# Two graph attention layers in one kernel: h1 stored by columns, deeper h and output buffers, an earlier start of the sparse rows

## The reference

```
h  = relu(layernorm(x))                       # layer 0
Wh = h @ W
e  = (Wh @ a[:256])[:, None] + (Wh @ a[256:])[None, :]
x  = x + leaky_relu(softmax(where(adj == 0, -1e9, e), axis=1) @ Wh, 0.2)
h  = relu(layernorm(x))                       # layer 1
h1, h2 = h @ a1[:256], h @ a1[256:]
e  = leaky_relu(h1 + h2.T, 0.01)
x  = x + softmax(where(adj > 0, e, -9e15), axis=1) @ h
```

## Time and profile before

| | |
|---|---|
| median of three runs | 1716.38 us |
| profiled execution | 1716.22 us |
| its span | 1714.0 us |
| end of layer 0, start of layer 1 | 1068.7 us |
| busy over the span | PE 91%, DVE 73%, ACT 58%, POOL 33% |
| mean granted TensorE clock | 0.966 of full speed |

### The profile page before, as it was taken

One profiled execution on the slowest core, in us unless ns is written; L12 is line 12 of the kernel. 1 busy time (PEld: TensorE's weight loads), 2 busy tenths in 40 slices (PEclk: granted clock), 3 DMA queues, 4 the chain that ended last, 5 costly groups with the idle time before them and its releaser, 6 DMA issues. The chain is left out here.

```text
span 1714.0 us, 37172 instructions
## 1 busy us (share of the span) xinstructions
PE 1559.3 (91%) x13443; PEld 1327.4 (77%) x13443; DVE 1258.1 (73%) x4759; ACT 992.5 (58%) x1514; POOL 557.3 (33%) x588
## 2 busy tenths in 40 slices
PE   6877999999999999999999997585599999899877
PEld 5646888888888888888888886464488888787666
DVE  7577998998899889987864443596676766666556
ACT  5878656665666566657666641675454444444342
POOL 0000000000000000000035561576677777777774
PEclk9998999999999999999999999897799999999989
DMA  9418989988988898889899973745444444444433
GB/s 315 165 44 346 352 299 340 345 309 306 363 329 298 311 367 318 299 316 377 325 343 398 388 277 79 165 133 143 111 133 123 129 117 133 116 139 117 127 110 91
DMA packets 141698, 406.89 MB, mean 237 GB/s; under 512 B 25857, under 2 KB 91586, under 8 KB 108834
## 3 DMA queue, kind: packets, MB, share of 16 engines
q1 hardware_dynamic: 116114, 335.11, 53.5%
q0 software_dynamic: 25488, 70.77, 14.8%
HBM read 365.39 MB, written 40.41 MB: 237 GB/s over the span
## 5 line engine op out<-in xcount | busy, mean ns | idle before, releaser
L1006 PE MATMUL banks<-HV,adjT 128*128 128x257 f16 x8192 | 940.0, 274 | 16.6 <-DVE adjT L665 9.1
L1006 PEld LDWEIGHTS banks<-HV,adjT 128*128 128x128 fp8e4 x8192 | 793.3, 98 | 148.5 <-DVE HV L695 22.9
L1746 PE MATMUL banks<-Vp,adjp 128*128 128x257 f16 x2304 | 454.2, 279 | 97.2 <-DVE adjp L1560 79.8
L450 ACT ACTIVATE adj_f<-adj_i 128x2048 fp8e4<-128x2048 int32 x256 | 480.2, 1897 | 5.4 <-DMA adj_i<-in_adj 5.1
L1331 POOL DMA_INDIRECT gat<-h_of_layer,rec x393 | 415.0, 1056 | 149.3 <-issue 111.4
L1746 PE MATMUL banks<-Vn,adjn 128*128 128x257 f16 x2304 | 453.6, 279 | 0.0
L1746 PEld LDWEIGHTS banks<-Vp,adjp 128*128 128x128 fp8e4 x2304 | 226.0, 99 | 142.7 <-DVE Vn L1520 64.9
L432 POOL DMA_DIRECT2D xr<-x_after_layer x46 | 26.3, 572 | 832.4 <-DVE rank L933 772.3
L1746 PEld LDWEIGHTS banks<-Vn,adjn 128*128 128x128 fp8e4 x2304 | 228.8, 99 | 37.9
L1367 ACT ACTIVATE adjn<-h1bc,nh 128x384 fp8e5<-128x384 f32 x384 | 205.0, 605 | 35.5 <-PE banks L1746 31.1
L1619 DVE SCALAR_TENSOR_TENSOR sacc<-gat,w,sacc 128x257 f32<-128x257 f32 x347 | 156.7, 478 | 0.0
(11 more groups left out here) (172 smaller groups left out, 1484.3 us busy)
## 6 DMA issues: line engine op xcount, KB each, us to landing
adj_i<-in_adj SPq DMA_DIRECT2D x256, 1024.0 KB, 7.0
h_of_layer<-hh SPq DMA_DIRECT2D x64, 129.0 KB, 6.3
hs<-h_of_layer SPq DMA_DIRECT2D x64, 129.0 KB, 2.7
xt<-in_x SPq DMA_DIRECT2D x64, 128.0 KB, 6.7
packed_adj<-pk SPq DMA_DIRECT2D x64, 128.0 KB, 6.1
x_after_layer<-x SPq DMA_DIRECT2D x64, 128.0 KB, 6.6
HV<-in_x SPq DMA_DIRECT2D x14, 512.0 KB, 8.8
gat<-h_of_layer,rec POOLq DMA_INDIRECT x393, 2.8
```

What stands on the lines that cost most here:

```text
L450: nc.scalar.activation(adj_f[:, b, q * QC:(q + 1) * QC], adj_i[:, q, :], ACT.Copy, scale=2.0, saturate=False).then_inc(conv_done, 1)
L1006: last = nc.tensor.matmul(acc[b][:, 0:DV], adjT_h[:, b, i, q, :, h], V0[:, jb, s, 0:DV], start=(jb == 0 and s == 0), stop=(jb == T - 1 and ...
L1746: mm = nc.tensor.matmul(bank[2 * i + part][:, 0:DV], m[:, i * P:(i + 1) * P], V[:, j, s, 0:DV], start=(j == 0 and s == 0), stop=(j == T - ...
```

## The change

In layer 0 `store_h` also stores the tile's column of `h1all`, 128 numbers from 128 partitions, to its row of `h1_d`; layer 0 ends only when all 64 have landed. Layer 1 has no transpose, copy and store of h1 any more; its first transfer is the broadcast of h1 for group 0. `HS` goes from 4 to 8: eight tiles of h are loaded at the start (two share a semaphore), and later ones two chunks ahead instead of one. `NOUT` goes from 4 to 6. `HEAD` goes from 1.0 to 0.25, so three rows stand in the loop of chunk 1 and five in those that follow. For chunk 0 the low halves and the weights of the own rows come before the first masks, and ACT's Exp for those weights before the first signs; for later chunks the order stays.

```diff
                 def store_h(t, off, b):
                     sp.wait_ge(h12_kept, 3 * t + 3)
                     sp.dma_start(h_rows(t + off), hh[:, b, :]).then_inc(hh_out[b], 16)
+                    sp.dma_start(h1_d[t + off, :].rearrange("(p o) -> p o", o=1), h1all[:, t + off:t + off + 1])\
+                        .then_inc(h1_out, 16)
...
                 sp.wait_ge(rec_in, 16)
+                sp.wait_ge(h1_out, 16 * T)
...
-        HS = 4
+        HS = 8
...
-        HEAD = 1.0
+        HEAD = 0.25
         OUT_LAG = 5
-        NOUT = 4
+        NOUT = 6
...
-                for b in range(HS):
-                    sp.dma_start(hs[:, b, :], h_rows(tiles[b])).then_inc(h_in[b], 16)
+                load_h1(0, 0)
+                for b in range(CB):
+                    sp.dma_start(hs[:, b, :], h_rows(tiles[b])).then_inc(h_in[b // 2], 16)
                 load_words(0, 0)
+                for b in range(CB, HS):
+                    sp.dma_start(hs[:, b, :], h_rows(tiles[b])).then_inc(h_in[b // 2], 16)
                 load_words(0, 1)
-                sp.wait_ge(h1T_sb, 1)
-                sp.dma_start(h1_d, h1T[:, :]).then_inc(h1_out, 16)
-                sp.wait_ge(h1_out, 16)
-                load_h1(0, 0)
                 load_h1(1, 1)
...
-                    if g == 0 and c < NC - 1:
-                        for t in range((c + 1) * CB, (c + 2) * CB):
+                    if g == 0:
+                        for t in range(c * CB + HS, min(T, (c + 1) * CB + HS)):
                             sp.wait_ge(v_ready, 2 * (t - HS) + 2)
-                            sp.dma_start(hs[:, t % HS, :], h_rows(tiles[t])).then_inc(h_in[t % HS], 16)
+                            sp.dma_start(hs[:, t % HS, :], h_rows(tiles[t])).then_inc(h_in[t % HS // 2], 16)
...
                 halves(0)
+                act.wait_ge(wself_ready, 2)
+                nc.scalar.activation(zself[:, :, :], zself[:, :, :], ACT.Exp).then_inc(wself_ready, 1)
                 signs_of(0)
                 signs_of(1)
                 halves(1)
                 act.wait_ge(hb_ready, 2)
-                act.wait_ge(wself_ready, 2)
-                nc.scalar.activation(zself[:, :, :], zself[:, :, :], ACT.Exp).then_inc(wself_ready, 1)
...
-                nc.vector.tensor_copy(h1T[:, :], bank[7][0:T, 0:P]).then_inc(h1T_sb, 1)
...
+                    if n == 0:
+                        for t in range(CB):
+                            low_halves(t, t % HS)
+                        self_weights()
                     negatives(n, g, c)
-                    if g == 0:
-                        low_halves(c * CB, 0)
+                    if g == 0 and n > 0:
+                        low_halves(c * CB, c * CB % HS)
                     positives(n, c)
-                    if g == 0:
+                    if g == 0 and n > 0:
...
                 prepare(0)
-                self_weights()
...
-                nc.tensor.transpose(bank[7][0:T, 0:P], h1all[:, :], idf[:, :]).then_inc(h1T_ps, 1)
```

More of the change, by code:

```diff
@@ L302, in two_layer_graph_attention @@
             rec_in = sem("rec_in")
+            h1_out = sem("h1_out")
             x1_out = [sem(f"x1_out{i}") for i in range(NX)]
@@ L1118, in two_layer_graph_attention @@
             tM = early[:, 6 * T:7 * T]
-            h1T = early[0:T, 7 * T:7 * T + P]
             sS = early[:, 9 * T:9 * T + 2 * NS].rearrange("p (s t) -> p s t", s=2)
@@ L1143, in two_layer_graph_attention @@
             fac = cnt[:, 4 * G:6 * G].rearrange("p (s g) -> p s g", s=2)
-            h_in = [sem(f"h_in{i}") for i in range(HS)]
+            h_in = [sem(f"h_in{i}") for i in range(HS // 2)]
             pkg_in = [sem(f"pkg_in{i}") for i in range(2)]
@@ L1148, in two_layer_graph_attention @@
             x1g_in = sem("x1g_in")
-            h1T_ps = sem("h1T_ps")
-            h1T_sb = sem("h1T_sb")
-            h1_out = sem("h1_out")
             exc_ready = sem("exc_ready")
@@ L1348, in _ @@
                 act.wait_ge(dM_ready, 2)
-                act.wait_ge(h1T_ps, 1)
                 nc.scalar.activation(ab[:, :, :], dM[:, :, :], ACT.Exp).then_inc(ab_ready, 1)
@@ L1353, in high_halves @@
                 def high_halves(t, j, n_in):
-                    act.wait_ge(h_in[j], n_in)
+                    act.wait_ge(h_in[j // 2], n_in)
                     for s, V in ((0, Vp), (1, Vn)):
@@ L1409, in halves @@
                     for j in range(CB):
-                        high_halves(c * CB + j, j % HS, (c * CB + j) // HS * 16 + 16)
+                        t = c * CB + j
+                        high_halves(t, t % HS, t // HS * 32 + 32)
                 def signs_of(n):
@@ L1462, in _ @@
             def _(dve):
+                nc.vector.tensor_scalar(nh2[:, :], h2all[:, :], -BIG, None, ALU.mult)\
+                    .then_inc(nh2_ready, 1)
                 nc.vector.tensor_tensor(exc[:, :], rec_f[:, :, DEG], capv[:, :], ALU.subtract).then_inc(exc_ready, 1)
@@ L1467, in _ @@
                 nc.vector.reduce_max(red_in[:, 2:3], exc[:, :], AX.X).then_inc(mx_ready, 1)
-                dve.wait_ge(h1T_ps, 1)
-                nc.vector.tensor_copy(h1T[:, :], bank[7][0:T, 0:P]).then_inc(h1T_sb, 1)
-                nc.vector.tensor_scalar(nh2[:, :], h2all[:, :], -BIG, None, ALU.mult)\
-                    .then_inc(nh2_ready, 1)
                 dve.wait_ge(M_all, 1)
@@ L1661, in prepare @@
                         unpack(n, g, c, n >= 2 * UB)
+                    if n == 0:
+                        for t in range(CB):
+                            low_halves(t, t % HS)
+                        self_weights()
                     negatives(n, g, c)
-                    if g == 0:
-                        low_halves(c * CB, 0)
+                    if g == 0 and n > 0:
+                        low_halves(c * CB, c * CB % HS)
                     positives(n, c)
-                    if g == 0:
-                        for j in range(1, CB):
-                            low_halves(c * CB + j, j % HS)
+                    if g == 0 and n > 0:
+                        for t in range(c * CB + 1, c * CB + CB):
+                            low_halves(t, t % HS)
                 def self_weights():
@@ L1737, in group @@
                                     if j == 0:
-                                        if first and i == 0 and part == 0:
-                                            pe.wait_ge(h1T_sb, 1)
                                         if not first:
```

## The result

The changed kernel takes **1805.0 us** (median of four runs, 1794.97 to 1810.58), 1.0508 times the kernel before on the same chip [1.046, 1.0555]. Forecast were 1687.3 us. The change is slower by 5%, and the prediction is wrong.

What follows compares the result with a forecast made beforehand. The prediction took POOL to bound layer 1 from 1232 to about 1690 us, with PE full in layer 0's fullest stretch. From 1716.22 us, -27.2 + 8.2 + 0.7 - 2.6 - 8 = -28.9 gave 1687.3 us, range 1672 to 1704.

Steps and rivals of the forecast that it cites:

- The cost in layer 0: Layer 0's 64 added column stores: taken as 0 because PE never waits, upper bound 7 us.
- The end of layer 0: Last column store is one issue and one landing later than the last h: +0.7 us (0.4 to 1.5).
- if layer 0 ends more than 2 us later: Sign at the end of layer 0 that would show the forecast wrong.
- POOL's stops: Layer 1's first group: POOL's seven stops for DVE to free a gather buffer go away, -27.2 us.
- Rows from chunk 0: Layer 1's first group: earlier rows and eight h buffers remove POOL's 10.98 us stop.
- SyncE's blocks: Layer 1's first group: output buffer waits at L1226 stay, but the third holds nothing up; DVE loses some 10 and 4 us.
- The others under 8: Sign in layer 1's first group: ACT's 16.5 us wait for h gone, its other waits under 8 us.
- The price of the fuller DVE: Layer 1's first group: gathers take longer beside a denser DVE, +8.2 us.
- The rival with 2.5 us for a gather and its gap: Layer 1's first group: DVE's unbroken runs block POOL throughout, ending at 1728.9 us; chance 5%.
- The start and the change of group: Layer 1: PE starts some 1.5 us earlier, and its group 1 at 1200 to 1208 us instead of 1232.
- The tail: End of layer 1: six output buffers remove two late POOL stops, -2.6 us, and bring the last sums earlier, -8 us.
- the likeliest case: Whole kernel: the forecast itself, 1687.3 us with its own range 1678 to 1698; chance 65%.

Runs made afterwards that it cites:

- e6: Kernel before plus one extra store per layer 0 tile, 128 pieces of 32 bytes without gaps; 1714.37 us, ratio 0.9992.
- e4: Kernel before plus one extra store per layer 0 tile, 128 pieces of 512 bytes without gaps; 1712.65 us, ratio 0.9996.
- e10: Kernel before plus one extra store per layer 0 tile, 128 pieces of 4 bytes, 32 bytes apart; 1712.68 us, ratio 0.9998.
- e2: Changed kernel without the column stores; h1 goes to DRAM through the transpose on PE, as before; 1685.86 us, ratio 0.9843.
- e9: As e2, but with four h buffers (HS 4) as before; 1699.07 us, ratio 0.9896.
- e8: As e2, but with HEAD 1.0 as before; 1686.72 us, ratio 0.984.
- e7: As e2, but with four output buffers (NOUT 4) as before; 1695.24 us, ratio 0.989.
- e15: Kernel before plus a store per layer 0 tile: 128 4-byte pieces filling one 512-byte row, neighbours written 16 pieces apart; 1766.34 us, ratio 1.0309.
- e1: Kernel before plus the column store of h1 in layer 0, 128 pieces of 4 bytes without gaps per tile; 1809.14 us, ratio 1.0543.
- e16: Kernel before plus a store per layer 0 tile: 128 4-byte pieces without gaps, from 16 partitions; 1882.93 us, ratio 1.0989.

## Why the prediction was wrong, step by step

- **The cost in layer 0 is the step that failed:** "I take 0, by the PE row", with an upper bound of 7 us. It asked what the 128 pieces take by themselves, at the mean packet of that queue, 1.0 us per engine and tile, and held that against PE's 50.00 of 50. In place of 0 the last product of layer 0 came 104.6 us later (1165.8 instead of 1061.2). The runs show 53.6 us of engine time per tile ((0.627 x 16 x 1804.3 - 0.535 x 16 x 1714.0) / 64), 3.35 us per engine, and it lies in other packets: 50.3 of it in the 8 KB packets of the adjacency. The second error is in the cover. The bound counted seven tiles, those of the fullest stretch; at a share of 0.88 a store that takes twice what is free makes nearly every tile late. PE at 50.00 of 50 said that PE was not waiting yet, not how much room the transfers had: the share of 1.01 in the same row was the warning.
- *The page beside it.* The Trainium skill (DMA: Bandwidth & Descriptors, "Specifications") gives 512 bytes as the least size for full rate. The traces agree that small pieces move at a lower rate: by the packet records a 32-byte piece of e6 took 8.9 ns, a 512-byte piece of e4 27.5 and an undisturbed 8 KB packet 309, which is 3.6, 18.6 and 26.5 bytes per ns. The 14 us estimated from the page were too little all the same, and falling under 512 bytes is not what costs here: 128 pieces of 32 bytes without gaps (e6) cost 2.2 us of engine time, 128 of 512 bytes (e4) 2.3, and 4-byte pieces 32 bytes apart (e10) 2.2.
- **The end of layer 0:** +0.7 us was forecast, and 21.3 us passed from the last product to the start of layer 1 instead of 7.5. SyncE stood up to 38.7 us for the sort's scatters at L397 (22.7 before), and five stores of h and five of columns were issued behind it, from 1169.64 us on. In e2, without the columns, layer 1 starts at 1068.7 us again. The prediction's own sign, "if layer 0 ends more than 2 us later", came true by 118.5 us.
- **POOL's stops, -27.2 us, were right** in size: 2.1 us of stops are left in e2, 1.7 in the kernel after. The mechanism was right for the eight h buffers (e9: 32.0 us of stops with four). The step "Rows from chunk 0" credited the first stop to `HEAD` and the buffers together. It is just as gone in e8, with late rows and eight buffers (no stop over 2.2 us), and in e9, with early rows and four, that gather waits 2.26 us. So `HEAD` adds nothing that shows to the eight buffers; what the new order of chunk 0 gives, no run takes apart.
- **SyncE's blocks** stay, as forecast (75.3 us in four waits in e2), and POOL doesn't run dry behind them. "The others under 8" failed for ACT's waits: one of 11.7 us is left in e2, and POOL did not stop for it.
- **The price of the fuller DVE, +8.2 us, was too high.** 68 gathers took 88.25 us in e2, 1.30 each and 1.60 with the gap of 0.30; the forecast had (16.9 + 93.4) / 66 = 1.67 over the same stretch, so some 5 us too much. All 393 gathers together agree: 418.1 us against 415.0, +3.1. The rival with 2.5 us for a gather and its gap did not come. The Trainium skill (SBUF — State Buffer, "Who interferes with whom") has the later of two contending VectorE and GpSimd instructions blocked for the whole instruction; a mean of 1.30 us neither shows nor excludes that for single gathers.
- **The start and the change of group:** PE starts group 1 at 1204.46 (forecast 1200 to 1208).
- **The tail, -2.6 - 8 = -10.6 us, was about right:** e7 measures 8 to 9.4. From the end of the last gather to the sums it is 7.9 us (1666.09 to 1673.98) instead of 15.4; 6.4 were forecast. ACT's waits for an output buffer shrink from 55.3 to 2.0 us in e2.
- **The sum without the column store** would have been 1686.6 us. e2's 0.9843 on the median of 1716.38 is 1689.4, inside the likeliest case's own range. It came near in part because errors offset. In e2's profiled run POOL's last gather ended 24.8 us earlier (1666.09 instead of 1690.87), where -27.2 + 8.2 - 2.6 gives 21.6, and what follows the sums took 9.5 us (to the span's 1683.5) instead of 7.7. None of the rivals had the place of the loss: the slower one was put in layer 1.

## What to carry to other kernels

Price a small store by what it does to the transfers behind it, not by its own bytes alone, and look for the stretch in which the DMA share is near one: there is no cover there, however full the engine is that hides the rest. Bring numbers that lie one per partition into a row (here a transpose on the matrix engine, with one store for all 64 tiles) before they go to DRAM; where they must go by columns, 32 bytes from piece to piece made the store harmless here. And when a busy engine is offered as the proof that transfers are hidden, read how much of the transfers' own time is free.

## What the runs showed of the hardware

- 128 pieces of 4 bytes without gaps kept the 16 DMA engines busy for about 6 us at 152 to 169 GB/s instead of 408, at a busy share of 0.90 to 0.96 (1.01 at the 408): a busy share alone doesn't tell the rate.
- The same pieces 8 bytes apart cost half of that engine time (23.2 of 49.9 us), 32 bytes apart a twentieth (2.2).
- The same row of 512 bytes cost 38.8, 49.9 or 64.4 us of engine time (e15, e1, e16), by the order and the partitions from which it was written.
